# Products of constants behind the first scores of an attention and in the last step of two stacks

## The chip, the cores and the metric

The kernel runs as one program on one core of a Trainium2 chip. The metric is the device time of one execution in microseconds, the median over several runs. TensorE (PE in the rows) does the products and transposes, VectorE (DVE), ScalarE (ACT) and GpSimd (POOL) the rest; SyncE (SP) issues the transfers. TensorE's clock has two levels, 1.2 and 2.4 GHz; the profile gives it as a share of the upper one (0.50 or 1.00).

## The reference

A stream x of 8 sequences of 256 tokens by 128 features goes through four levels. Each level adds half of a feed-forward part, then an attention, then half of the same feed-forward part again:

```python
x = x + 0.5 * ffn(layernorm(x)); x = x + attn(layernorm(x)); x = x + 0.5 * ffn(layernorm(x))
```

Two parts matter here. The feed-forward part of level 2 is itself a stack of six layers, run twice in the program, before and after the attention of level 2:

```python
for i in range(6):
    x = attn_layer(shift_tokens(x), ...) + x      # 16 heads of 64, local windows of 32
    x = ffn_layer(shift_tokens(x), ...) + x       # (a * gelu(gate)) @ W2, width 341
```

The attention of level 2 is a softmax attention over all 256 tokens with 16 heads of 8 features:

```python
h = (x - mu) * rsqrt(var + 1e-5) * gamma + beta
q, k, v = split(h @ w_qkv + b_qkv)
attn = softmax(q @ k.T / sqrt(8))
out = residual + (attn @ v) @ w_out + b_out
```

## The kernel before

Twelve stages run one after the other, each in a block of its own, and every engine has its own instruction list, written in a fixed order by hand; semaphores tie them together. All numbers are float32. A float32 product is two matmul records in the trace; a transpose is one.

**stage_attention, level 2.** A step is one batch of 256 tokens, two tiles of 128. The eight batches are software-pipelined: `body(s)` on PE interleaves steps s-3 to s+1. Per step PE turns the normalized x (`turn_normed`, L915), projects q and k (`project`, L923) and v (`project_v`, L937), and computes the scores twice. The first scores, `first_score(step, g)` for four groups g of four heads (L963), write the PSUM tile `quad`; DVE reduces each group to the maxima, `reduce`, L1722, and as there is one `quad`, group g + 1 waits for the reduction of g. PE turns the maxima (`turn_negmax`, L980, into the tile `turn`, which the copy of v, L1683, must have left), DVE adds them to the queries (`q_aug`, L1738), and `score(step, n)`, n = 0 to 7 (L1005), writes the scores turned into the tile `duo`, two heads at a time. ACT takes the exponential of each (L1448) before the next may overwrite `duo`. `weigh` (L1024) multiplies by v; turns and the output product follow.

Three places already hold products of constants, whose result nobody reads. `warm(n)` (L973) multiplies the identity by itself n times into `duo`; it stands as `warm(6)` ahead of the loop and as `warm(1)` in each place of `body(0)` whose operation has no batch yet. `fill(n)` (L969) does it into `quad`: six times behind the turn of the maxima of the last batch, once behind each score of the last batch. `first_score(0, g)` is thus followed by the places of absent operations: eight records behind group 0, for instance. In `body(1)` the order around group 3 is `first_score(0, 3)`, `project_v(1)`, `turn_negmax(0)`, `first_score(1, 0)`, `score(0, 0)`.

**stage_stack.** A step is one batch in one layer, 48 steps, software-pipelined over four; `tail()` writes out the last four by hand. The last step's feed-forward part has nothing beside it: `output(last)` (L2847, 16 records), `turn_out(6)` (L2890, two transposes of batch 6 that leaves the stack), `to_tokens(last)` (L2854) once DVE has added the residual into `zc`, DVE and POOL for the statistics and the normalized `fxn`, `turn_normed(last)` (L2860), ACT for `fxnT` and the load of gelu's table, then for each of three chunks `up` (L2872), gelu on ACT (L3204), a multiplication on DVE (L3655), and `down` (L2879), whose result leaves through `turn_out(7)` (L2890) to x on DVE (L3671). The PSUM tile `score_psum` is not used any more at that point. `up`'s next chunk waits for the multiplication of the one before.

Of the kernel before, what the change touches and what calls it, by code (L numbers as in the profile page):

```python
# [21 lines left out]
P = 128  # L22
D = 128
B, SEQ = 8, 256
# [820 lines left out]
def stage_attention(chip, level):  # L845
    nc, sig, once = chip.nc, chip.loop, chip.once
# [9 lines left out]
    with ExitStack() as ctx:  # L856
        sb = lambda name, shape, dt=F32: ctx.enter_context(nc.sbuf_tensor(chip.tag + name, shape, dt))
        ps = lambda name, shape: ctx.enter_context(nc.psum_tensor(chip.tag + name, shape, F32))
        pack = sb("pack", [P, sum(width for _, width in ATTN_PARTS[level])])
        tiles = views(pack, ATTN_PARTS[level])  # L860
        if not softmax:
# [42 lines left out]
        def _(pe):  # L904
# [35 lines left out]
            def first_score(step, g):  # L940

                if softmax and g % 2 == 0:
                    pe.wait_ge(*sig("heads", step, g // 2 + 1))
                elif g == 0:
                    pe.wait_ge(*sig("k_heads", step, 1))
                pe.wait_ge(*sig(drained, step, g))
                if cut:
                    for j in range(GROUPS):
                        nc.tensor.matmul(kinds2(quad[:, j, :])[:, :, 0:P], ident_bf[:, :],
                                         mask[:, :].rearrange("p (o s) -> p o s", o=1).to_broadcast([P, T, P]),  # L950
                                         start=True, stop=False, skip_group_check=True)
                for t in range(T):
                    for j in range(GROUPS):
                        band = slice(BAND * j, BAND * (j + 1))
                        if softmax:
                            query, key = q_heads[band, step % ROOM, g, :], k_heads[band, step % ROOM, g, :]
                        else:
                            query, key = flat[band, step % ROOM, 0, :], k_heads[band, step % ROOM, 0, g, :]
                        if cut:
                            ins = nc.tensor.matmul(quad[:, j, t * P:(2 * t + 1) * P], query[:, t * P:(t + 1) * P],  # L960
                                                   key[:, 0:(t + 1) * P], start=False, stop=True, skip_group_check=True)
                        else:
                            ins = nc.tensor.matmul(quad[:, j, t * SEQ:(t + 1) * SEQ], query[:, t * P:(t + 1) * P], key,  # L963
                                                   start=True, stop=True, skip_group_check=True)
                ins.then_inc(sig["first_scores"], 1)

            def fill(count):
                for n in range(count):
                    nc.tensor.matmul(quad[:, n % GROUPS, 0:P], chip.ident[:, :], chip.ident[:, :], start=True, stop=True, skip_group_check=True)  # L969
# [5 lines left out]
            def turn_negmax(step):  # L975
                if step == 0:
                    pe.wait_ge(*once("set", 1))
                pe.wait_ge(*sig("negmax", step, GROUPS))
                for t in range(T):
                    ins = nc.tensor.transpose(turn[:, t * P:(t + 1) * P], negmax[:, t, :], chip.ident[:, :])  # L980
                ins.then_inc(sig["negmaxT"], 1)
                if step == B - 1:
                    fill(6)

            def score(step, n):
# [65 lines left out]
            if level == 0:  # L1051
                def body(s):
# [20 lines left out]
                    if runs(s + 1):  # L1073
                        bank_free(("xT", s + 3, 1), ("context", s - 1, 1))
                        turn_negmax(s + 1)
                    elif s == -2:
                        warm(1)
                    if runs(s + 2):
                        first_score(s + 2, 0)
                    elif s == -2:  # L1080
                        warm(1)
# [19 lines left out]
                    if runs(s + 2):  # L1101
                        first_score(s + 2, 1)
                    elif s == -2:
                        warm(1)
# [24 lines left out]
                    if runs(s + 2):  # L1129
                        first_score(s + 2, 2)  # L1130
                    elif s == -2:
                        warm(1)
# [34 lines left out]
            elif level == 2:  # L1167
                def body(s):
# [38 lines left out]
                    if runs(s - 1):  # L1207
                        bank_free(("v", s, 1), ("ctxT", s - 3, 1))
                        turn_negmax(s - 1)
                    elif s == 0:  # L1210
                        warm(1)
# [1331 lines left out]
def stage_stack(chip):  # L2543
# [9 lines left out]
    nc, dram, att, layer_sig, once = chip.nc, chip.dram, chip.loop, chip.layer, chip.once  # L2553
    once.use(dict(set=3, loaded=64, tables=DEPTH, primed=2))
    with ExitStack() as ctx:
# [33 lines left out]
        wide, score_psum = ps("wide", [P, 2, 512]), ps("score_psum", [P, 2, 512])  # L2589
# [165 lines left out]
        def _(pe):  # L2755
# [84 lines left out]
            def output(step):  # L2840


                pe.wait_ge(*att("ctxT", step, 4))
                pe.wait_ge(*att("z", step + B))
                pe.wait_ge(*layer_sig("wo", layer_of(step), 16))
                for c in range(LPAIRS):
                    ins = nc.tensor.matmul(out_psum, wo[:, c, :], ctxT[:, c, :], start=c == 0, stop=c == LPAIRS - 1)  # L2847
                ins.then_inc(att["out_psum"], 1)

            def to_tokens(step):  # L2850

                pe.wait_ge(*att("zc", step, 2))
                for t in range(HALVES):
                    ins = nc.tensor.transpose(f_psum[:, t * P:(t + 1) * P], zc[:, t * P:(t + 1) * P], chip.ident[:, :])  # L2854
                ins.then_inc(att["fxs_psum"], 1)

            def turn_normed(step):
                pe.wait_ge(*att("xn", step, 1))
                for t in range(HALVES):
                    ins = nc.tensor.transpose(f_psum[:, t * P:(t + 1) * P], fxn[:, t, :], chip.ident[:, :])  # L2860
                ins.then_inc(att["fxnT_psum"], 1)

            def up(step, c):

                if c == 0:
                    pe.wait_ge(*att("fxnT", step, 1))
                    pe.wait_ge(*layer_sig("ffn", layer_of(step), 48))
                else:
                    pe.wait_ge(*att("hidden", step, c))
                for half in range(2):  # L2870
                    at = half * FF + c * P
                    ins = nc.tensor.matmul(up_psum[0:width(c), half, :], w1[:, at:at + width(c)], fxnT[:, :], start=True, stop=True)  # L2872
                ins.then_inc(att["h_psum"], 1)

            def down(step):

                pe.wait_ge(*att("hidden", step, FF_CHUNKS))
                for c in range(FF_CHUNKS):
                    ins = nc.tensor.matmul(out_psum, w2[0:width(c), c, :], hidden[0:width(c), c, :],  # L2879
                                           start=c == 0, stop=c == FF_CHUNKS - 1)  # L2880
                ins.then_inc(att["f_psum"], 1)

            def turn_out(b):
                if b == 0:
                    pe.wait_ge(*att("v", STEPS - 1, HALVES))
                pe.wait_ge(att["leave"], att.base["leave"] + b + 1)
                if b > 1:
                    pe.wait_ge(att["left"], att.base["left"] + b - 1)
                for t in range(HALVES):
                    ins = nc.tensor.transpose(wide[:, b % 2, t * P:(t + 1) * P], straight[:, b % 4, t * P:(t + 1) * P], chip.ident[:, :])  # L2890
                ins.then_inc(att["tok"], 1)
# [94 lines left out]
            def tail():  # L2986
# [66 lines left out]
                turn_probs(second, 3)  # L3053
                weigh(second, 2)
                turn_out(0)
                turn_normed(third)
                turn_out(1)
                turn_free(("qkT", last, 4))
                turn_qk(last, 4)
                turn_out(2)  # L3060
                up(third, 0)
                turn_out(3)
# [46 lines left out]
                weigh(last, 7)  # L3109
                output(last)  # L3110
                turn_out(6)
                to_tokens(last)
                turn_normed(last)
                up(last, 0)
                up(last, 1)
                up(last, 2)
                down(last)
                turn_out(7)

# [3 lines left out]
            with pe.Fori(2, STEPS - 2) as s:  # L3123
                body(s)
            tail()

        @block.scalar
# [851 lines left out]
```

## Time and profile before

| what | us |
|---|---|
| median of 3 runs | 5163.54 |
| lowest and highest | 5163.06, 5172.06 |
| the profiled execution | 5160.11 |
| its span in the trace | 5158.3 |
| PE busy | 4911.5 |
| DVE busy | 3883.5 |
| ACT busy | 3435.8 |
| POOL busy | 2884.5 |

The span runs from the first to the last instruction. Busy times overlap, and a busy PE isn't one at its peak: a record's length depends on the granted clock. The idle time in brackets in a timeline is that of the engine in front of the instruction, with what it waited for.

### The profile page before, as it was taken

The numbers are of one execution on the slowest core, as the hardware profiler recorded it, in microseconds if no ns is written. First come the engines' busy times: TensorE is split into PE (matmuls) and PEld (weight loads), VectorE is DVE, ScalarE is ACT, GpSimd is POOL, SyncE is SP. The second block draws the span as 40 slices with busy tenths as digits, with TensorE's granted clock in tenths as the row PEclk, the third lists the DMA queues.
The fourth block names the chain that finished last, engine by engine and source line by source line (L and its number), as shares of the span: only waits on it lengthen the run. The fifth ranks groups of instructions, "written<-read, shape, count | busy, mean of one in ns | idle before, by whom it ended". The sixth has DMA issues, their size and how long they took to land. (4 is left out here: it accounts for less than half of the span.)

```text
span 5158.3 us, 142024 instructions
## 1 busy us (share of the span) xinstructions
PE 4911.5 (95%) x49396; PEld 3459.2 (67%) x49396; DVE 3883.5 (75%) x7068; ACT 3435.8 (67%) x5890; POOL 2884.5 (56%) x3477
## 2 busy tenths in 40 slices
PE   9989988699999999999979699999999999989999
PEld 6666656377777777777756377777777777756656
DVE  3274347699999999999856489989999989855655
ACT  3353334488888888888846478888888888852652
POOL 0010025688888888888720488888887888720200
PEclk9999999799999999999979799999999999989999
DMA  1000000112121112111100112111211111110000
GB/s 45 1 6 35 1 8 3 53 40 61 43 61 49 51 49 56 53 53 52 40 16 2 42 45 57 49 55 47 57 53 51 51 54 53 40 42 1 8 26 9
DMA packets 110503, 195.62 MB, mean 38 GB/s; under 512 B 21456, under 2 KB 28896, under 8 KB 110304
## 3 DMA queue, kind: packets, MB, share of 16 engines
q1 hardware_dynamic: 110304, 192.89, 13.3%
q8 instruction: 134, 2.20, 0.2%
q14 instruction: 65, 0.53, 0.0%
HBM read 53.36 MB, written 1.05 MB: 11 GB/s over the span
## 5 line engine op out<-in xcount | busy, mean ns | idle before, releaser
L3433 POOL TENSOR_TENSOR stage_qk<-stage_halves 128x1024 f32<-128x1024 f32 x384 | 907.7, 2364 | 17.0 <-DVE stage_halves L3591 1.9
L3469 POOL TENSOR_TENSOR stage_qk<-stage_qk,stage_rnorm 128x1024 f32<-128x1024 f32 x384 | 730.5, 1902 | 8.1 <-POOL stage_rnorm L3458 0.2
L3462 POOL TENSOR_TENSOR stage_probs<-stage_probs,stage_rsum 128x768 f32<-128x768 f32 x384 | 564.4, 1470 | 263.9 <-DVE stage_rsum L3620 263.9
L3184 ACT ACTIVATE stage_probsT<-stage_flip 96x512 f32<-96x512 f32 x768 | 452.3, 589 | 219.2 <-PE stage_flip L2821 218.5
L3588 DVE TENSOR_TENSOR stage_halves<-stage_wide,stage_tables 128x1024 f32<-128x1024 f32 x384 | 469.3, 1222 | 145.1 <-ACT stage_square L3138 94.2
L3591 DVE TENSOR_TENSOR stage_halves<-stage_wide,stage_tables 128x512 f32<-128x512 f32 x768 | 490.7, 680 | 0.0
L3600 DVE TENSOR_REDUCE stage_norm<-stage_square 128x16 f32<-128x1024 f32 x384 | 463.8, 1208 | 32.4 <-issue 32.3
L3138 ACT ACTIVATE stage_square<-stage_wide 128x1024 f32<-128x1024 f32 x384 | 393.2, 1024 | 141.1 <-PE stage_wide L2769 136.4
L2786 PE MATMUL stage_turn<-ident,stage_qk 128*128 128x128 f32 x3072 | 480.6, 279 | 6.5 <-ACT stage_qkT L3158 6.5
L2821 PE MATMUL stage_flip<-ident,stage_probs 128*96 128x128 f32 x3072 | 469.5, 275 | 7.9 <-POOL stage_probs L3462 6.9
L2835 PE MATMUL stage_pv<-stage_probsT,stage_v_win 96*64 96x64 f32 x12288 | 464.8, 226 | 2.5 <-ACT stage_ctxT L3191 1.5
L3158 ACT ACTIVATE stage_qkT<-stage_turn 128x512 f32<-128x512 f32 x768 | 454.3, 592 | 15.9 <-PE stage_turn L2786 14.1
L2835 PEld LDWEIGHTS stage_pv<-stage_probsT,stage_v_win 96*64 96x64 f32 x12288 | 397.7, 138 | 90.3 <-issue 86.3
L2821 PEld LDWEIGHTS stage_flip<-ident,stage_probs 128*96 128x96 f32 x3072 | 343.4, 126 | 167.0 <-issue 79.6
L2786 PEld LDWEIGHTS stage_turn<-ident,stage_qk 128*128 128x128 f32 x3072 | 353.9, 142 | 139.0 <-issue 85.4
L707 DVE SCALAR_TENSOR_TENSOR stage_mixes<-stage_o_psum,stage_routes,stage_mixes 128x128 f32<-128x128 f32 x480 | 135.2, 344 | 347.5 <-PE stage_o_psum L529 320.0
L3611 DVE TENSOR_TENSOR stage_shifted<-stage_score_psum,stage_negmax 128x768 f32<-128x768 f32 x384 | 367.6, 957 | 36.5
L2769 PE MATMUL stage_wide<-stage_wq,stage_xsT 128*128 128x512 f32 x768 | 380.2, 618 | 11.6 <-DVE stage_halves L3591 7.3
L2769 PE MATMUL stage_wide<-stage_wk,stage_xsT 128*128 128x512 f32 x768 | 372.6, 609 | 17.7 <-DVE stage_halves L3591 17.6
L529 PEld LDWEIGHTS stage_o_psum<-stage_w_down,stage_hidden 128*128 128x128 f32 x3072 | 359.6, 192 | 42.0 <-issue 41.1
L516 PE MATMUL stage_h_psum<-stage_xT,stage_w_up 128*128 128x512 f32 x768 | 384.0, 612 | 1.8 <-DMA stage_w_down<-in_L_w_down 1.1
L2769 PE MATMUL stage_wide<-stage_wv,stage_xsT 128*128 128x512 f32 x768 | 369.0, 604 | 7.8 <-DVE stage_halves L3591 5.5
(311 smaller groups left out, 10017.7 us busy)
## 6 DMA issues: line engine op xcount, KB each, us to landing
stage_v_win<-stage_v SPq DMA_DIRECT2D x384, 192.0 KB, 2.5
stage_v_win<-stage_v SPq DMA_DIRECT2D x384, 128.0 KB, 2.4
stage_v_win<-stage_v SPq DMA_DIRECT2D x192, 64.0 KB, 2.2
stage_wq<-in_T_wq SPq DMA_DIRECT2D x12, 512.0 KB, 4.1
stage_wk<-in_T_wk SPq DMA_DIRECT2D x12, 512.0 KB, 4.8
stage_wv<-in_T_wv SPq DMA_DIRECT2D x12, 512.0 KB, 3.4
stage_wo<-in_T_wo SPq DMA_DIRECT2D x12, 512.0 KB, 3.5
stage_w_up<-in_L_w_up SPq DMA_DIRECT2D x8, 512.0 KB, 7.1
```

What stands on the lines that cost most here:

```text
L2769: ins = nc.tensor.matmul(wide[:, c, :], xsT[:, (n % HALVES) * P:(n % HALVES + 1) * P], weights[name][:, c * 512:(c + 1) * 512], start=True ...
L2786: ins = nc.tensor.transpose(turn[:, j * P:(j + 1) * P], qk[:, chunk, pair * P:(pair + 1) * P], chip.ident[:, :])
L2821: ins = nc.tensor.transpose(flip[0:REACH, (2 * h + t) * P:(2 * h + t + 1) * P], probs[:, (n // 2) % 2, h, (n % 2) * HALVES + t, :], chip.i ...
L2835: ins = nc.tensor.matmul(pv[h * LD:(h + 1) * LD, n % 2, block * QBLOCK:(block + 1) * QBLOCK], v_win[:, block, 2 * n + h, :], probsT[:, n % ...
L3158: nc.scalar.activation(target, tiles4(turn), ACT.Copy).then_inc(att["qkT"], 1)
L3184: nc.scalar.activation(probsT[:, n % 2].rearrange("p h t q -> p (h t) q"), tiles4(flip)[0:REACH], ACT.Copy)\
L3433: nc.gpsimd.tensor_tensor(qk[:, n, :], halves[:, n % 2, 0, :], halves[:, n % 2, 1, :], ALU.add)\
L3462: nc.gpsimd.tensor_tensor(probs[:, m % 2], probs[:, m % 2], rsum[:, m % 2].to_broadcast([P, 2, 2 * HALVES, REACH]), ALU.mult)\
L3469: nc.gpsimd.tensor_tensor(heads, heads, rnorm[:, n, :].rearrange("p (h o) -> p h o", o=1).to_broadcast([P, LH, LD]), ALU.mult).then_inc(at ...
L3588: nc.vector.tensor_tensor(out[:, 0], heads, cos.to_broadcast([P, LH, LD]), ALU.mult)
L3591: ins = nc.vector.tensor_tensor(out[:, 1, :, to], heads[:, :, source], sin[:, :, to].to_broadcast([P, LH, LD // 2]), ALU.mult)
L3600: nc.vector.tensor_reduce(norm2[:, n, :], square[:, n % 2, :].rearrange("p (h d) -> p h d", d=LD), AX.X, ALU.add)\
```

## The change

Three edits, all of them added products of the identity by itself. In the attention of level 2, for the first batch only, `warm` runs 6, 2, 8 and 8 times behind the four groups of first scores, and `fill(6)` behind the turn of its maxima, as it did for the last batch. In the stack a function `fill` of the same kind, into `score_psum`, is called six times in the last step of `tail()`, 25 products in all.

```diff
@@ stage_attention, PE: first_score(step, g)
                 ins.then_inc(sig["first_scores"], 1)
+                if level == 2 and step == 0:
+                    warm((6, 2, 8, 8)[g])
@@ stage_attention, PE: turn_negmax(step)
                 ins.then_inc(sig["negmaxT"], 1)
-                if step == B - 1:
+                if step == B - 1 or level == 2 and step == 0:
                     fill(6)
@@ stage_stack, PE
+            def fill(count):
+                for n in range(count):
+                    nc.tensor.matmul(score_psum[:, n % 2, 0:P], chip.ident[:, :], chip.ident[:, :], start=True, stop=True, skip_group_check=True)
@@ stage_stack, PE: tail()
                 turn_out(6)
+                fill(4)
                 to_tokens(last)
+                fill(10)
                 turn_normed(last)
+                fill(3)
                 up(last, 0)
+                fill(3)
                 up(last, 1)
+                fill(3)
                 up(last, 2)
+                fill(2)
                 down(last)
                 turn_out(7)
```

## Rows read from the trace of the kernel before

**Rows 1.** The page: busy time by engine, and the granted clock in 40 slices.

```profile
PE 4911.5 (95%) x49396; PEld 3459.2 (67%) x49396; DVE 3883.5 (75%) x7068; ACT 3435.8 (67%) x5890; POOL 2884.5 (56%) x3477
...
PEclk9999999799999999999979799999999999989999
```

**Rows 2.** Busy time in stretches: length, each engine's busy us, PEclk, DMA share, GB/s.

```profile
2624.00:2640.00 16.00, 9.77 (x20) 5.37 (x20) 3.14 (x7) 4.96 (x7) 0.00 (x0) 0.50 0.00 0
...
2668.00:2712.00 44.00, 38.84 (x221) 23.61 (x220) 22.01 (x40) 14.12 (x19) 4.36 (x7) 0.50 0.00 1
...
4576.00:4593.00 17.00, 9.77 (x20) 5.38 (x20) 3.14 (x7) 5.15 (x8) 0.69 (x1) 0.50 0.00 0
```

**Rows 3.** Timeline, last step of the first stack: start, length, instruction, records, idle before.

```profile
2620.49 0.38 PE L2890 MATMUL stage_wide<-ident,stage_square 128*128 128x128 f32 x2
...
2621.62 0.44 PE L2854 MATMUL stage_f_psum<-ident,stage_zc 128*128 128x128 f32 x2 [0.75 <-DVE stage_zc L3628]
...
2624.78 0.69 PE L2860 MATMUL stage_f_psum<-ident,stage_fxn 128*128 128x128 f32 x2 [2.72 <-DVE stage_fxn L3647]
...
2626.09 1.28 ACT L3204 ACT_TABLE_LOAD   x1
...
2626.12 2.07 PE L2872 MATMUL stage_f_psum<-stage_fxnT,stage_w 128*128 128x256 f32 x4 [0.65 <-ACT stage_fxnT L3198]
...
2635.58 2.93 PE L2879 MATMUL stage_f_psum<-stage_hidden,stage_w 128*128 128x256 f32 x6 [1.08 <-DVE stage_hidden L3655]
...
2640.48 0.69 PE L2890 MATMUL stage_wide<-ident,stage_square 128*128 128x128 f32 x2 [1.97 <-ACT stage_square L3216]
```

**Rows 4.** The same timeline of PE, the same products one step earlier.

```profile
2609.43 1.03 PE L2872 MATMUL stage_f_psum<-stage_fxnT,stage_w 128*128 128x256 f32 x4
...
2614.05 1.56 PE L2879 MATMUL stage_f_psum<-stage_hidden,stage_w 128*128 128x256 f32 x6
```

**Rows 5.** Timeline of PE and DVE, level 2 attention, first batch.

```profile
2642.16 2.90 PE L973 MATMUL stage_duo<-ident 128*128 128x128 f32 x12 [1.00 <-PEq L2555]
...
2659.33 1.15 PE L963 MATMUL stage_quad<-stage_k_heads,stage_q_heads 32*128 32x256 f32 x16 [1.39 <-DVE stage_negmax L1722]
...
2660.68 1.06 PE L973 MATMUL stage_duo<-ident 128*128 128x128 f32 x8
...
2662.99 1.15 PE L963 MATMUL stage_quad<-stage_k_heads,stage_q_heads 32*128 32x256 f32 x16 [0.29 <-DVE stage_negmax L1722]
...
2666.54 1.15 PE L963 MATMUL stage_quad<-stage_k_heads,stage_q_heads 32*128 32x256 f32 x16 [1.76 <-DVE stage_negmax L1722]
...
2667.75 2.29 DVE L1722 TENSOR_REDUCE stage_negmax<-stage_quad 128x8 f32<-128x2048 f32 x1 [0.28 <-PE stage_quad L963]
...
2669.96 0.41 DVE L1683 TENSOR_TENSOR stage_v<-stage_turn,stage_pack 128x256 f32<-128x256 f32 x1
...
2670.43 0.69 PE L980 MATMUL stage_turn<-ident,stage_negmax 128*128 128x128 f32 x2 [1.79 <-DVE stage_v L1683]
...
2672.91 1.92 PE L1005 MATMUL stage_duo<-stage_q_aug,stage_k_heads 32*128 32x256 f32 x8
...
2675.95 0.80 PE L1005 MATMUL stage_duo<-stage_q_aug,stage_k_heads 32*128 32x256 f32 x2 [1.12 <-ACT stage_probs L1448]
...
2685.49 2.08 PE L923 MATMUL stage_pvT<-stage_xT,stage_pack 128*128 128x256 f32 x4
...
2692.40 0.80 PE L1005 MATMUL stage_duo<-stage_q_aug,stage_k_heads 32*128 32x256 f32 x2 [1.12 <-ACT stage_probs L1448]
```

**Rows 6.** Timeline of PE, level 2 attention, scores of the last batch.

```profile
2845.62 1.13 PE L1005 MATMUL stage_duo<-stage_q_aug,stage_k_heads 32*128 32x256 f32 x8
...
2847.88 1.25 PE L1005 MATMUL stage_duo<-stage_q_aug,stage_k_heads 32*128 32x256 f32 x8 [0.70 <-ACT stage_probs L1448]
...
2850.64 2.08 PE L1005 MATMUL stage_duo<-stage_q_aug,stage_k_heads 32*128 32x256 f32 x8
```

**Rows 7.** Timeline of PE, level 0 attention, a score of the first batch.

```profile
297.11 0.92 PE L1005 MATMUL stage_duo<-stage_q_aug,stage_k_heads 32*128 32x256 f32 x8 [0.91 <-ACT stage_probs L1448]
```

## The prediction, made before the changed kernel ran

> **What bounds the kernel now.** I read the page first, for the share of each engine and the row of the granted TensorE clock [rows 1]. TensorE is busy 95% of the span, so where its work is dense its speed sets the time. The clock row is below 9 tenths in a few slices only; I took those apart with the view by stretches [rows 2], then followed the instructions in order of time through the three places that the diff touches: the last step of each stack, and the first batch of the level 2 attention.
>
> Two kinds of lost time stand there. First, the end of a stack: in 2624 to 2640 and again in 4576 to 4593 the granted clock is 0.50, the lower of the two levels, 1.2 GHz [rows 2]. That step is one chain: a product, an activation, a vector operation, the next product, nothing beside it, so each product at half speed lengthens the program by its excess. Second, the attention: the clock is at 0.50 from about 2668 to 2712, with PE busy 38.84 of the 44 us [rows 2]. Around 2668 the engine had done little: it had idled 1.76 us in front of the fourth group of first scores and 1.79 us in front of the turn of the maxima [rows 5]. Before the fall in the stack it had idled 0.75 us, done two turns, and was in a pause of 2.72 us [rows 3].
>
> **The price of a filler.** One product of a filler is two records of a 128x128 float product. At half level 12 records take 2.90 us, at full level 8 take 1.06 us with the pipeline's tail [rows 5]; without the tail (0.42 and 0.27) that is about 0.22 and 0.11 us a record, so 0.43 and 0.23 us a filler.
>
> **The stacks' last step.** It gets 25 fillers, 50 records, in six places, all in pauses.
> - fill(4), 0.91 us at full level, starts behind the two turns issued at 2620.49, so near 2620.71, and ends near 2621.62, exactly where to_tokens started when DVE released it [rows 3]. Cost 0, with nothing to spare.
> - fill(10), 2.3 us, goes into the pause of 2.72 us [rows 3]: cost 0.
> - fill(3) before up 0: 0.68 us into 0.65 us of pause and the 0.25 us by which the turns shorten. fill(3) twice and fill(2) before up 1, up 2 and down: 0.68, 0.68 and 0.46 us into pauses of 1.1 us, as in front of down [rows 3]. Cost 0 at full level.
>
> What they buy is the full level for what follows. The same products at full level stand a few microseconds earlier [rows 4]: the two turns 0.44 for 0.69, four records of up 1.03 for 2.07, six of down 1.56 for 2.93 [rows 3]. So: turns 0.25; up 0 1.04, but the load of the activation table (1.28 us, 2626.09 to 2627.37) is now late next: it starts with the turns' 0.25 us gain at 2625.84, ends at 2627.12, and holds the gelu that began at 2628.23, so turns and up 0 together give 1.1; up 1 and up 2 about 1.0 each, down 1.37, the last turn 0.25. Sum 4.7 us. If the last turn, which stands behind two more microseconds of idle, is back at half level, 4.5. Two stacks: 9.2 us. Bounds: nothing if the level falls all the same, 9.4 if it holds to the end.
>
> **The attention's start.** All of it moves 4.7 us earlier. Its head runs at half level today up to about 2654 and I leave that; whether the level comes back a little earlier or later against the work is open, for the products that run meanwhile (about six fillers and a projection) ±1 us. I put +0.5.
>
> **More products behind first scores.** The four groups are spaced by first score, reduction of 2.29 us on DVE, next first score. warm(6) behind group 0 is 12 records, 1.37 us, in a pause of 1.39 us plus the tail of the old eight (0.27): cost 0. warm(2) behind group 1, 0.46 us, delays project(1), but PE had 0.29 us and the tail before group 2 [rows 5]: at most 0.1. warm(8) behind group 2, 1.83 us, in 1.76 us plus 0.27: 0 to 0.1. warm(8) behind group 3 is in front of project_v(1): its four records now start 1.8 us later, at 2669.4, and end near 2670.0, where the copy of v on DVE began at 2669.96 [rows 5] behind the reduction. Cost 0.1 or 0.2, since the turn of the maxima waits for that copy. fill(6), 1.37 us, stands in front of first_score(1, 0), and so of its reduction, and of score(0, 0); with turn and first_score at full level (0.4 and 1.15 us, against 2.5 us now from turn to score) score(0, 0) starts at about 2673.2 instead of 2672.91. So nothing is won up to here, 0.3 lost.
>
> **Behind them.** Now it counts how long the level holds. The scores of batch 0 go through one pair of banks: score, a pause of 1.12 us for the exponential, next score [rows 5]; a score at full level is 1.13 us, as in rows 6. So score(0, 0) at 2673.2, score(0, 1) at 2675.4 (was 2675.95, 0.6 won). first_score(1, 1) and a turn, 2.3 us with it, cover the next wait: score(0, 2) at 2677.7, score(0, 3) at 2679.9, project(2) at 2680.9 (was 2685.49, 4.6 won). project(2) 1.0, first_score(1, 2) 1.1 and score(0, 4) 1.1 reach 2684.0, and a pause 2685.1 with score(0, 5) (was 2692.40, 7.3 won). Between these scores stand pauses of about 1.2 us, in front of scores 1, 3 and 5, with no filler in them, and a score uses 32 of the 128 rows. The nearest row: late in the same attention, at full level, two scores with a filler and a pause of 0.70 us between them, and the level falls within the second (1.25 us; the next one 2.08) [rows 6]. Against it: in the level 0 attention a pause of 0.91 us between two such scores, and they stay short [rows 7]. The pauses here are longer than both. So the likeliest is that the level falls again in one of them; I take the middle one, 4.6 us, ends 0.6 and 7.3. From there the work is at half level as before, and comes back where it does now.
>
> The Trainium skill (TensorE: Matmul & The Clock Gate, section A second HAM failure mode: psum-queue depth-cycling) says that small idle times between groups of matmuls that cycle through PSUM buffers make the gate swing between its levels. By that rule the scores of the first batch fall again, as rows 6 show once. The same page's closing table (Why this matters for your kernels) asks only that no long idle stand between bursts; by that rule today's fall near 2668, with no pause above 1.79 us [rows 5], would not be there, so the trace disagrees; it would give the second rival's time.
>
> **Sum.** -9.2 (stacks), +0.5 (start), +0.3 and -4.6 (first batch) is -13.0 us. On the profiled execution, 5160.11 us (its span 5158.3 and 1.8 around it), that is 5147. The median of the runs, 5163.54, is 3.4 above the profiled one, so 5150.5; I predict 5150.
>
> **Rivals.**
> 1. *The level falls again among the first batch's scores* (the forecast): 5150, own range 5145 to 5155. Chance 0.50.
> 2. *It holds into the steady state.* 2668 to 2712 has 38.8 us of busy PE at half level [rows 2] and 5 us idle; at full level 19.4, with 1.4 for fill(6), three pauses of 1.2 and some 2.5 of start and tails: 27 for 44, so -17 less 0.3. With the stacks -25: 5138. For it: rows 7. Against it: rows 6. Chance 0.22.
> 3. *Little arrives.* The level falls in the stack's end despite fill(4) and fill(10), in one or both, or the head of the attention stays at half level beyond the fillers; half of the 9.2 and none to 4 us of the rest remain: 5154 to 5161, within 0.2%. For it: fill(4) has no time to spare and the level was already gone by 2624. Chance 0.20.
> 4. *The fillers run at half level and become the wait.* Then each costs 0.43 us. Behind the first scores: 2.6 less 1.4 of pause, 0.9 less 0.3, 3.4 less 1.8, 3.4 with almost none, and 2.6 for fill(6): about 10 us. In the stack 1.7 less 0.75, 4.3 less 2.7, 1.3 less 0.65, 1.15 and 1.08: about 3.4 us each. Together +17, 5180; the attention's part alone, with the stacks as forecast, gives about 5164. It decides if the level isn't back when group 1 is issued, and in both stacks is gone before fill(10). Against it: the first scores run at full level today (1.15 us a group) [rows 5]. Chance 0.05.
> The other 0.03 is effects on later stages, whose own changes of level shift with everything.
>
> **From this the numbers.** A change within 0.2%, 10.3 us, is about what can't be told from none. Faster by more: most of case 1 (0.43 of 0.50; its low end, -9.8, is just inside the bound) and all of case 2: 0.65. Within: the rest of case 1, case 3, and part of the rest: 0.29. Slower: 0.06. Range 5137 to 5160, from case 2 to most of case 3.
>
> **What would show it.** In the profile after: a granted clock near 1.00 over the 16 us in front of each stack's last turn, up at 1.03 to 1.13 us and down at 1.56 (step right), or 2.07 and 2.93 (case 3). The four first-score groups of batch 0 still 3.6 us apart, else the fillers are the wait (case 4). project_v(1) followed at once by the copy of v. Then the length of each score(0, n): 1.13 turning to 2.08 at score 1, 3 or 5 is case 1, 1.13 throughout case 2. Wrong, too, if half-level stretches move elsewhere: a tail that ends 4.7 us sooner and a later stage that gives it back.

## The result: 18 us less in the first comparison, 0.35%

| | us |
|---|---|
| before, median of 6 | 5164.16 (5163.06 to 5172.06) |
| changed, median of 6 | 5146.01 (5136.93 to 5151.52) |
| ratio, 95% interval | 0.9965 [0.9952, 0.9978] |
| the changed kernel's profiled execution, its span | 5140.83, 5139.0 |

The page of the changed kernel, the lines that answer to [rows 1]:

```profile
PE 4909.0 (96%) x49556; PEld 3465.6 (67%) x49556; DVE 3883.5 (76%) x7068; ACT 3437.8 (67%) x5890; POOL 2884.5 (56%) x3477
...
PEclk9999999799999999999999799999999999999999
```

PE is busy 2.5 us less with 160 records more (49556 for 49396): 80 products of constants were added, 30 in the attention and 25 in each stack, and others got shorter. The stretches, as in [rows 2], same columns:

```profile
2624.00:2640.00 16.00, 11.93 (x77) 9.87 (x75) 5.32 (x15) 5.38 (x8) 0.69 (x1) 1.00 0.00 1
2641.00:2655.00 14.00, 8.34 (x35) 7.35 (x36) 8.02 (x32) 3.77 (x9) 7.91 (x10) 0.52 0.12 36
...
2668.00:2712.00 44.00, 39.38 (x410) 26.92 (x409) 31.66 (x56) 25.25 (x36) 5.88 (x9) 1.00 0.01 1
4556.00:4573.00 17.00, 12.56 (x80) 10.48 (x78) 5.33 (x15) 5.38 (x8) 0.69 (x1) 1.00 0.00 0
```

Both stacks' ends and the 44 us from 2668 on are at full level in this execution. A short stretch at half level stays between them, in the head of the attention (2641 to 2655, 0.52).

The timeline of PE in the last step of the first stack, as [rows 3]:

```profile
2620.43 3.72 PE L2849 MATMUL stage_f_psum<-stage_ctxT,stage_wo 128*128 128x256 f32 x16 [0.70 <-ACT stage_ctxT L3203]
...
2624.20 1.06 PE L2887 MATMUL stage_score_psum<-ident 128*128 128x128 f32 x8
2625.12 0.44 PE L2856 MATMUL stage_f_psum<-ident,stage_zc 128*128 128x128 f32 x2
2625.39 2.40 PE L2887 MATMUL stage_score_psum<-ident 128*128 128x128 f32 x20
2628.27 0.44 PE L2862 MATMUL stage_f_psum<-ident,stage_fxn 128*128 128x128 f32 x2 [0.48 <-DVE stage_fxn L3659]
...
2629.37 1.13 PE L2874 MATMUL stage_f_psum<-stage_fxnT,stage_w 128*128 128x256 f32 x4
...
2631.74 1.13 PE L2874 MATMUL stage_f_psum<-stage_fxnT,stage_w 128*128 128x256 f32 x4 [0.58 <-DVE stage_hidden L3667]
...
2636.12 1.56 PE L2881 MATMUL stage_f_psum<-stage_hidden,stage_w 128*128 128x256 f32 x6 [0.63 <-DVE stage_hidden L3667]
2639.65 0.44 PE L2896 MATMUL stage_wide<-ident,stage_square 128*128 128x128 f32 x2 [1.96 <-ACT stage_square L3228]
```

In it, up takes 1.13 us where it took 2.07, down 1.56 for 2.93, and the last turn 0.44 for 0.69. From the start of output(last) to the start of the last turn it takes 19.22 us, and took 23.55.

The timeline of PE in the first batch of the attention, as [rows 5]:

```profile
2655.68 1.15 PE L963 MATMUL stage_quad<-stage_k_heads,stage_q_heads 32*128 32x256 f32 x16
2656.76 2.50 PE L975 MATMUL stage_duo<-ident 128*128 128x128 f32 x20
2659.30 1.15 PE L963 MATMUL stage_quad<-stage_k_heads,stage_q_heads 32*128 32x256 f32 x16
...
2666.64 1.15 PE L963 MATMUL stage_quad<-stage_k_heads,stage_q_heads 32*128 32x256 f32 x16
2667.72 2.05 PE L975 MATMUL stage_duo<-ident 128*128 128x128 f32 x16
...
2670.74 0.44 PE L982 MATMUL stage_turn<-ident,stage_negmax 128*128 128x128 f32 x2 [0.52 <-DVE stage_v L1685]
2671.01 1.50 PE L971 MATMUL stage_quad<-ident 128*128 128x128 f32 x12
...
2673.41 1.03 PE L1007 MATMUL stage_duo<-stage_q_aug,stage_k_heads 32*128 32x256 f32 x8
2675.56 0.70 PE L1007 MATMUL stage_duo<-stage_q_aug,stage_k_heads 32*128 32x256 f32 x4 [1.12 <-ACT stage_probs L1450]
...
2680.11 1.13 PE L1007 MATMUL stage_duo<-stage_q_aug,stage_k_heads 32*128 32x256 f32 x8 [1.12 <-ACT stage_probs L1450]
2681.17 1.13 PE L923 MATMUL stage_pvT<-stage_xT,stage_pack 128*128 128x256 f32 x4
```

The first two groups of first scores still start 3.62 us apart (2655.68, 2659.30): the products behind them lie in the pauses. Pauses of 1.12 us for the exponential stand in front of scores 1, 3 and 5, and no score gets longer: in this execution the level holds.

Split at landmarks that both traces have, the profiled executions differ by 19.3 us:

| from, to | before | changed | difference |
|---|---|---|---|
| start, output(last) of the first stack | 2616.93 | 2620.43 | +3.50 |
| to the last turn of that stack | 23.55 | 19.22 | -4.33 |
| to the turn of the maxima of batch 0 | 29.95 | 31.09 | +1.14 |
| to the turn of the maxima of batch 2 | 58.80 | 42.43 | -16.37 |
| to output(last) of the second stack | 1840.12 | 1840.24 | +0.12 |
| to its last turn | 23.93 | 19.61 | -4.32 |
| to the end of the span | 565.02 | 565.98 | +0.96 |

The first row holds no changed instruction. That executions of one kernel differ by microseconds in places that nobody touched is what the experiments had to deal with. Over the 14 profiled executions of this document the first output(last) starts anywhere from 2613.62 to 2631.73 us, and the stretch from the turn of the maxima of batch 2 to output(last) of the second stack takes 1835.15 to 1848.01 us, with no edit in either but e8's in the last batch. These differences are larger than any that the edits make, so single times of whole executions don't decide between the theories below; the intervals between landmarks do.

### The profile page after: what moved, and what is told of

It is laid out like the page before. It is cut to its first block and busy times, and to the rows that moved or that the text cites. A ratio compares the mean times of both kernels' runs of the same rounds, so it can differ in the third digit from the quotient of the medians.

```text
span 5139.0 us, 142344 instructions
## 1 busy us (share of the span) xinstructions
PE 4909.0 (96%) x49556; PEld 3465.6 (67%) x49556; DVE 3883.5 (76%) x7068; ACT 3437.8 (67%) x5890; POOL 2884.5 (56%) x3477
## 3 DMA queue, kind: packets, MB, share of 16 engines
q1 hardware_dynamic: 110304, 192.89, 13.4%
```

## The experiments

Two intervals are compared over all of them, read from the starts of the rows in each timeline: the **end** of a stack, from output(last) to the last turn, and the **first batches**, from the turn of the maxima of batch 0 to that of batch 2 (and to that of batch 1 where it is named). Each comes from one profiled execution and is a difference of two rounded starts, so 0.01 us means nothing. The expectations of e9 to e12 count from landmarks on DVE instead: their 21.5 and 16.9 us of a stack's end are the 23.55 and 19.22 here. Their 43.1 us, and the 25 to 28 us of the changed kernel in e12's, run from the first addition of the maxima (2671.21 in the first trace) to a reduction on DVE that starts at 2714.30. The last column is the median of the whole execution. Where it is of one run there is no verdict on the time. The runs come from three series, each with its own executions of before: median 5163.87 us of 34 for e1 to e4, 5159.89 of 19 for e5 to e8, one of 5164.18 for e9 to e12.

| kernel | end of stack 1 | end of stack 2 | first batches | us (runs) |
|---|---|---|---|---|
| before | 23.55 | 23.93 | 58.80 | 5164.16 (6) |
| e9, before again | 22.79 | 23.91 | 48.47 | 5150.91 (1) |
| e10, before a third time | 22.81 | 23.91 | 48.46 | 5150.55 (1) |
| e1, stacks only | 19.23 | 19.61 | 48.56 | 5150.41 (12) |
| e2, attention only | 23.56 | 23.64 | 44.08 | 5157.20 (12) |
| changed | 19.22 | 19.61 | 42.43 | 5146.01 (6) |
| e3, changed again | 19.23 | 19.61 | 44.08 | 5148.09 (12) |
| e4, pauses filled | 19.24 | 19.61 | 42.43 | 5141.34 (11) |
| e5, no fill(4), fill(10) | 20.42 | 20.55 | 44.08 | 5138.43 (1) |
| e6, no fill behind the maxima | 19.24 | 19.61 | 44.56 | 5147.75 (12) |
| e7, twice the stacks' fillers | 21.92 | 21.93 | 44.07 | 5153.42 (1) |
| e8, more places | 19.24 | 19.61 | 42.43 | 5139.49 (8) |
| e11, only fill(4), fill(10) | 19.23 | 21.88 | 44.07 | 5151.47 (1) |
| e12, only fill behind the maxima | 19.23 | 19.61 | 42.43 | 5136.44 (1) |

### e1 and e2: each part alone

e1 takes the attention's products out, e2 those of the stacks.

```diff
 e1, against the changed kernel
-                if level == 2 and step == 0:
-                    warm((6, 2, 8, 8)[g])
...
-                if step == B - 1 or level == 2 and step == 0:
+                if step == B - 1:
                     fill(6)
 e2, against the changed kernel: the six calls of fill in tail() removed
```

> Only the fillers in the last step of the two stacks; the level 2 attention as before. Theory A (each part by itself, as in the sum): 4.7 us for each stack at most, 4.3 as the trace after shows, so -8.6 to -9.4 us, 5154 to 5156. Theory B (the stacks' gain is given back by the attention's start, whose half-level stretch only ends later against the work): -4 or less, 5159 or more.

> Only the products behind the first scores and the maxima of the first batch of the level 2 attention; the stacks as before. Theory A (the level holds through the scores of the first batch in every execution): -15 us, 5149, in each run within 2 us. Theory B (it holds in some executions and falls again in others, as the prediction took for the likeliest): the runs spread over 10 us or more, the median between -5 and -12 us, 5152 to 5159.

e1: 5150.41 us median of 12, ratio to before 0.9983 [0.9970, 0.9995], which is 8.8 us of 5164 and what theory A expected. The ends are 19.23 and 19.61 us: both stacks win, in this execution too, and nothing of it is given back in the head (29.99 us from the last turn to the turn of the maxima, for 29.95). The median is below the expected 5154 and 13.5 us under before's (5163.87 of 34, from 5146.78 to 5173.51); the ratio isn't that of the medians, and its interval holds everything from 2.6 to 15.5 us. So the times agree with the 8.8 but don't measure it well; the ends of the stacks do.

e2: 5157.20 us median of 12, from 5147.11 to 5169.14, ratio 0.9991 [0.9978, 1.0004]: 4.6 us, alone not told from nothing. Theory A's 15 us lies outside the interval, which ends at 11.4; the size is theory B's, and its profile shows the level fall in the first batch. The spread of 22 us is not evidence for it: before itself spreads over 27. 8.8 and 4.6 make 13.4.

### e3: the changed kernel again

> The changed kernel once more, for another profiled execution and more times. Theory A (always holds): the same cold stretches in the attention as in the first trace, none between 2656 and 2832 us, times within 3 us of one another. Theory B (depends on the execution): times again spread over 10 us or more, and about half of the profiles show a score of the first batch that turns from 1.13 to 2.08 us behind a pause of 1.12 us.

5148.09 us median of 12, 5138.96 to 5162.23, ratio 0.9972 [0.9958, 0.9986], 14.5 us. That the level doesn't hold in every execution is theory B's: in the timeline of PE of this execution it falls, behind score 3 of batch 0:

```profile
2682.50 1.13 PE L1007 MATMUL stage_duo<-stage_q_aug,stage_k_heads 32*128 32x256 f32 x8 [1.12 <-ACT stage_probs L1450]
2683.56 1.49 PE L923 MATMUL stage_pvT<-stage_xT,stage_pack 128*128 128x256 f32 x4
2684.97 2.09 PE L963 MATMUL stage_quad<-stage_k_heads,stage_q_heads 32*128 32x256 f32 x16
2686.84 1.41 PE L1007 MATMUL stage_duo<-stage_q_aug,stage_k_heads 32*128 32x256 f32 x8
2689.38 0.48 PE L1007 MATMUL stage_duo<-stage_q_aug,stage_k_heads 32*128 32x256 f32 x2 [1.13 <-ACT stage_probs L1450]
```

score(0, 3) is still 1.13, project(2) is 1.49 and first_score(1, 2) 2.09 for 1.15, score(0, 4) 1.41, and the next is short again. So it falls behind two pauses of 1.12 us, as the prediction had it, but it is back within score(0, 4). The whole costs 1.65 us (44.08 for 42.43), not the rest of the way to the steady state. That is too little to make the spread of 23.3 us, which theory B laid to it: this execution's span is 11.8 us longer than the first one's, 7.8 of it between batch 2 and the second stack's last step and 3.1 ahead of the first stack's.

### e4: the pauses filled

```diff
 score(step, n), behind the increment of "scores"
+                if level == 2 and step == 0 and n in (0, 2, 4):
+                    pe.wait_ge(*(sig("xT", 2, 1) if n == 4 else sig("heads", 1, 2)))
+                    bank = turn if n == 4 else pvT.rearrange("p g s -> p (g s)")
+                    for i in range(4):
+                        nc.tensor.matmul(bank[:, 0:P], chip.ident[:, :], chip.ident[:, :], start=True, stop=True, skip_group_check=True)
```

> The changed kernel, and in the first batch four more products of constants behind scores 0, 2 and 4 (into banks that are free there), which take 0.9 of each pause of 1.12 us. Theory B (the pauses let the level fall in some executions): the spread of the times shrinks, and the median is 3 to 8 us below that of the changed kernel, 5138 to 5143. Theory A (it never falls there): the same as the changed kernel, 5146, or up to 0.5 us more for the added products.

5141.34 us median of 11, 5132.94 to 5149.69, ratio 0.9964 [0.9950, 0.9979]. The timeline of PE:

```profile
2681.06 1.03 PE L1007 MATMUL stage_duo<-stage_q_aug,stage_k_heads 32*128 32x256 f32 x8
2682.01 1.16 PE L1016 MATMUL stage_pvT<-ident 128*128 128x128 f32 x8
2683.21 0.70 PE L1007 MATMUL stage_duo<-stage_q_aug,stage_k_heads 32*128 32x256 f32 x4
```

Eight records fill the pause without delaying the next score, which again starts 2.15 us behind the one before, and the first batches take 42.43 us, the value without a fall. The median is 6.8 us under that of e3 and within what theory B expected, but the intervals of e3 and e4 overlap, and the fall that e4 avoids costs 1.65 us by the traces, so it can't be what makes the 6.8. Nor does the smaller spread (16.8 us for 23.3) say that the pauses made it: e6, with its pauses open, spreads over 15.1. What is shown is that filling the pauses costs nothing. In both executions with the pauses filled (e4, e8) the level held, and in one of the six with both edits and open pauses; that the filling makes the difference is likely, not shown.

### e9 and e10: the kernel before, two more executions

e1's unchanged attention had taken 48.56 us where the first trace of before had 58.80, which put the price of the whole attention part in doubt.

> The kernel before, once more, for another profiled execution. Theory A (the first trace is typical: the level is at half for some 44 us in the level 2 attention and 31 us from each stack's end): the first batch to the return of the level takes 43.1 us again, within 2. Theory B (how long the half level lasts there differs from one execution to the next, as the attention alone unchanged in e1 suggests, where it took 10.2 us less): another length, between 28 and 45 us; the stack's end 21.5 us again.

> The same again, a third execution. Theory B: the attention's stretch differs from the other two, while the stack's end stays at 21.5 us.

48.47 and 48.46 us; the stack's end 22.8 us, 0.75 less than in the first trace. The timeline of PE in e9:

```profile
2671.32 0.69 PE L980 MATMUL stage_turn<-ident,stage_negmax 128*128 128x128 f32 x2 [1.92 <-DVE stage_v L1683]
...
2686.38 2.08 PE L923 MATMUL stage_pvT<-stage_xT,stage_pack 128*128 128x256 f32 x4
2688.39 1.61 PE L963 MATMUL stage_quad<-stage_k_heads,stage_q_heads 32*128 32x256 f32 x16
2689.82 1.02 PE L1005 MATMUL stage_duo<-stage_q_aug,stage_k_heads 32*128 32x256 f32 x8
```

The level falls ahead of the turn of the maxima as in [rows 5] (0.69 us), already within the project_v(1) before it, and comes back within first_score(1, 2) (1.61 for 2.09), 17 us after the turn. In [rows 2] it stayed down for 44 us. Three executions of the unchanged attention (e9, e10, e1) take 48.5 us and one 58.8: what I read as the cost of the old schedule was, of these four, the longest. Theory B; but e9 and e10 do not differ from each other, and the end of the first stack did not stay as it was (22.8 for 23.55 us).

### e5, e7, e11: which filler of the stack does what

e5 drops fill(4) and fill(10), e11 drops the four later groups, e7 doubles all six.

```
 e5                      e11                     e7
-    fill(4)              (stays)                 fill(8)
-    fill(10)             (stays)                 fill(20)
     fill(3)             -    fill(3)             fill(6)
     fill(3)             -    fill(3)             fill(6)
     fill(3)             -    fill(3)             fill(6)
     fill(2)             -    fill(2)             fill(4)
```

> The changed kernel without fill(4) and fill(10) in the stacks' last step; fill(3), 3, 3 and 2 stay. Theory A (the two groups in front of the normalized x keep the level up, the others only fill): the level falls near the start of the statistics as before, up is 2.07 us again for at least the first chunk, and the products of constants at 0.43 us overrun their pauses: output(last) to the last turn takes 0 to 1 us more than before (23.5 us). Theory B (the four later groups are enough to bring the level back during up 0 or up 1): 1 to 3 us less than before, 20.5 to 22.5 us. The changed kernel took 19.2.

> The changed kernel without the four later groups in the stacks' last step; fill(4) and fill(10) stay. Theory A (the two early groups keep the level, and the chunks' own products carry it on): the end takes 16.9 us as in the changed kernel. Theory B (three chunks with pauses of 0.6 to 1.1 us between them let it fall again): up at 2.07 us from chunk 1 or 2 on, 18 to 20 us.

> The changed kernel with twice the products in the last step of the stacks: 8, 20, 6, 6, 6, 4. It prices a product at full level where no pause hides it. Theory A (0.22 us each, hidden only in what is left of each pause: 0, 0.48, 0, 0.58, 0.42, 0.63 us by the trace after): 0.9 + 1.8 + 0.7 + 0.1 + 0.3 = 3.8 us more per stack than the changed kernel, output(last) to the last turn 23.0 us. Theory B (products of constants are overlapped by the queue, or the level falls): under 2 us more, or over 6.

e5 takes 20.42 and 20.55 us. The timeline of PE, from the turn of the normalized x:

```profile
2628.81 0.69 PE L2862 MATMUL stage_f_psum<-ident,stage_fxn 128*128 128x128 f32 x2 [2.72 <-DVE stage_fxn L3657]
2629.29 1.48 PE L2887 MATMUL stage_score_psum<-ident 128*128 128x128 f32 x6
2630.57 1.73 PE L2874 MATMUL stage_f_psum<-stage_fxnT,stage_w 128*128 128x256 f32 x4
2632.14 0.83 PE L2887 MATMUL stage_score_psum<-ident 128*128 128x128 f32 x6
```

The level has fallen (turn 0.69, six records 1.48), but fill(3), up and fill(3) leave PE no pause, and it is back within up 0 (1.73). So the two early groups are worth 1.2 and 0.9 us on top of the later ones, which bring most of the gain alone: theory B, whose 20.5 to 22.5 us it meets within 0.1.

e11 takes 19.23 us in the first stack and 21.88 in the second. In the second, timeline of PE:

```profile
4572.31 1.13 PE L2874 MATMUL stage_f_psum<-stage_fxnT,stage_w 128*128 128x256 f32 x4 [1.24 <-DVE stage_hidden L3663]
4574.52 2.00 PE L2874 MATMUL stage_f_psum<-stage_fxnT,stage_w 128*85 128x256 f32 x4 [1.08 <-DVE stage_hidden L3663]
4577.60 2.93 PE L2881 MATMUL stage_f_psum<-stage_hidden,stage_w 128*128 128x256 f32 x6 [1.08 <-DVE stage_hidden L3663]
```

up 1 takes 1.13, up 2 takes 2.00: the level falls between them, behind pauses of 1.24 and 1.08 us. In one stack the early groups suffice, in the other they don't; with the later groups the level held in both stacks in all eight profiled executions that have the six groups (changed, e1, e3, e4, e6, e7, e8, e12). Each theory is right in one of the two stacks.

e7 takes 21.92 and 21.93 us, 2.7 and 2.3 more than the changed kernel. The timeline of PE:

```profile
2624.72 4.63 PE L2887 MATMUL stage_score_psum<-ident 128*128 128x128 f32 x40
2629.19 0.38 PE L2862 MATMUL stage_f_psum<-ident,stage_fxn 128*128 128x128 f32 x2
...
2637.34 1.56 PE L2881 MATMUL stage_f_psum<-stage_hidden,stage_w 128*128 128x256 f32 x6 [0.18 <-DVE stage_hidden L3667]
```

40 records take 4.63 us, 0.11 each, and delay the turn by what sticks out of the pause. In front of down 0.18 us of idle is left, so the last three groups stay hidden even when doubled. The sum expected by theory A was 3.8, and neither theory has 2.7 and 2.3. In the first stack 0.9 and 1.5 came at the first two groups (0.88, and 1.53 for 1.8), 0.46 at the third, and nothing after; up 0 gave 0.17 back. A filler at full level outside a pause costs 0.22 us, as priced.

### e6 and e12: the attention's two edits apart

```diff
 e6, against the changed kernel
-                if step == B - 1 or level == 2 and step == 0:
+                if step == B - 1:
                     fill(6)
 e12, against the changed kernel
-                if level == 2 and step == 0:
-                    warm((6, 2, 8, 8)[g])
```

> The changed kernel without fill(6) behind the maxima of the first batch; the 24 products behind the first scores stay. Theory A (the products behind the first scores carry the level over and fill(6) only stands in front of the next group): the first batch's scores start 1.1 to 1.4 us earlier and the level holds as often: 0 to 1.4 us faster than the changed kernel. Theory B (fill(6) is needed in the stretch of the turn of the maxima): the level falls more often in the pauses before scores 1 and 3, median 1 to 4 us slower than the changed kernel.

> The changed kernel without the 24 products behind the first scores; fill(6) behind the maxima stays. Theory A (the fall comes in the pauses of the first scores, so fill(6) is issued at half level and takes 2.6 us): the first batch to the steady state 25 to 28 us becomes 38 us or more, near the kernel before. Theory B (fill(6) brings the level back within one group): 28 to 33 us.

e6: 5147.75 us median of 12, ratio 0.9983 [0.9972, 0.9993], against e3's 0.9972 [0.9958, 0.9986], each to before of its own series: not told apart. Its stretches, columns as in [rows 2]:

```profile
2677.00:2681.00 4.00, 2.85 (x28) 1.86 (x30) 3.92 (x7) 1.02 (x1) 1.36 (x2) 1.00 0.00 0
2681.00:2685.00 4.00, 4.00 (x30) 2.85 (x30) 2.13 (x7) 1.31 (x2) 0.70 (x1) 0.57 0.01 4
...
2688.00:2692.00 4.00, 4.00 (x26) 2.88 (x26) 0.14 (x1) 2.95 (x5) 0.00 (x0) 0.57 0.00 0
```

The level falls twice (0.57 in 2681 to 2685 and in 2688 to 2692). score(0, 0) starts 1.46 us behind the turn, 1.2 sooner than with fill(6), and still the first batches take 44.56 us, 0.5 more than with one fall. A trade of 1.2 us for another fall of the level, in one execution.

e12 went against both expectations. The timeline of PE:

```profile
2659.24 1.15 PE L963 MATMUL stage_quad<-stage_k_heads,stage_q_heads 32*128 32x256 f32 x16 [1.76 <-DVE stage_negmax L1722]
...
2663.13 0.44 PE L980 MATMUL stage_turn<-ident,stage_negmax 128*128 128x128 f32 x2 [2.10 <-DVE stage_v L1683]
2663.40 1.50 PE L969 MATMUL stage_quad<-ident 128*128 128x128 f32 x12
```

With the old pauses, 1.76 us and 2.10 us, the turn is 0.44 us and fill(6) 1.50: the level had not fallen. The first batches take 42.43 us, the best value, without one of the 24 products behind the first scores. One execution doesn't tell how often; it shows that those products are not necessary each time. Nor can fill(6) have kept the level up to the turn, behind which it stands: ahead of the turn, e1 has the same instructions, and there it had fallen (0.69). What the products do shows over all profiled executions. With them the turn of the maxima takes 0.44 us in nine of nine (changed, e2 to e8, e11), e2 with the old stacks among them; without them 0.69 in four (before, e9, e10, e1) and 0.44 in one (e12).

### e8: more places

e4, and fill(3) for fill(1) behind scores 1 and 3 of the last batch, warm(15) for warm(6) ahead of the attention's loop, fill(6) between down and the last turn of each stack.

```diff
-                    fill(1)
+                    fill(3 if level == 2 and n in (1, 3) else 1)
...
-            warm(6)
+            warm(15 if level == 2 else 6)
...
                 down(last)
+                fill(6)
                 turn_out(7)
```

> The changed kernel with the pauses of the first batch filled as in e4, two more products behind scores 1 and 3 of the last batch, warm(15) for warm(6) ahead of the attention's loop, and fill(6) between down and the last turn of each stack. Theory A (each half-level stretch that is left near these places shortens): the last turn at full level in each stack, 0.2 us each; the attention's head 1 to 2 us shorter, since project(0) and the products behind it run at full level; the last batch without its stretch at half level, 1 to 7 us: median 2 to 6 us under e4's 5141.3. Theory B (the head is bound by VectorE and ScalarE and the last batch by the exponentials): the same as e4 within 2 us.

5139.49 us median of 8, 5129.68 to 5148.65, ratio 0.9962 [0.9948, 0.9975]: the lowest median, and not told apart from e4 or from the changed kernel. In its profile the scores of the last batch are all 1.13 us, with pauses of 0.26 where [rows 6] have 0.70. But e2, whose last batch is the old one with its pause of 0.70, shows the same; the sixth of the eight scores, in the timeline of PE of e2 and of e8:

```profile
2850.96 1.13 PE L1007 MATMUL stage_duo<-stage_q_aug,stage_k_heads 32*128 32x256 f32 x8 [0.27 <-ACT stage_probs L1450]
...
2845.29 1.13 PE L1007 MATMUL stage_duo<-stage_q_aug,stage_k_heads 32*128 32x256 f32 x8 [0.27 <-ACT stage_probs L1455]
```

From the first to the last of the eight scores it is 17.99 us in e2, e5 and e8, and 20.8 or 22.3 in the other eleven executions, where the sixth score takes 2.07 or 2.08. So holding the level there is worth at least 2.8 us, and it also comes without e8's products; whether they make it more frequent is open. The ends of the stacks and the first batches are those of e4, so neither fill(6) nor warm(15) shows anything; theory B for these two.

## Why the prediction was right, and where not

The time, 5146, lies in the range and in the direction that was forecast, 4 us under the 5150. The stacks' part came as worked out; that the attention's part brought the sum so near is luck, by two errors that cancel.

**The stacks' last step: right in mechanism and size.** 4.7 us a stack were worked out, 0.25 of it for the last turn itself. From output(last) to the start of the last turn 4.33 and 4.32 were won, and the turn shortened by the 0.25: 4.6. Against e9 and e10 the first stack wins 3.6 and not 4.3, as the level fell later there: its turn of the normalized x took 0.44 us. fill(4) does end where to_tokens starts (2625.12), the level stays up, and the activation table's load is the thing next late: up 1 comes 1.09 us sooner against the turn of the normalized x, where 1.1 was said. The timeline of ACT after, where gelu follows the load at once:

```profile
2629.33 1.28 ACT L3216 ACT_TABLE_LOAD   x1
2630.63 0.47 ACT L3216 ACTIVATE stage_gelu<-stage_f_psum,stage_cols 128x256 f32<-128x256 f32 x1
```

**The attention's head: right.** +0.5 with ±1 around it; +1.14 in this pair of traces; in the other executions the stretch takes 29.8 to 31.1 us, for 29.95 to 30.08 in the three of before. In the changed kernel's first trace the level came back later against the work, so project_v ran at 1.06 us and the last warm products at 1.22.

**The products behind the first scores: right as costs, and they do hold the level.** Groups 3.62, 3.78 and 3.56 us apart, the middle one 0.12 later as the 0.1 of the sum has it, project_v(1) followed at once by the copy of v, score(0, 0) 2.67 us behind the turn for 2.8. The turn of the maxima is at full level in nine of nine executions with them and in one of five without. The prediction names the 1.79 us in front of the turn as idle time before the fall, but the level had already gone in the project_v(1) ahead of that pause, as the timeline of PE before shows (1.02 us, 0.61 after):

```profile
2667.61 1.02 PE L937 MATMUL stage_turn<-stage_pack,stage_xT 128*128 128x128 f32 x4
```

So of the pauses named only the 1.76 us came before it.

**The chain behind them: right.** project(2) at 2681.17 is 7.76 us behind score(0, 0); 7.7 was worked out.

**The step that failed, although the time came right,** is "From there the work is at half level as before, and comes back where it does now." The level did fall in the pauses where the prediction put it: e3 shows it, and e2, e5, e7 and e11 have the same length, 44.07 or 44.08 us. That is five of the six profiled executions with both edits of the attention and nothing in its pauses; the sixth, the first one, held. But the level came back within a few microseconds, and a fall cost 1.65 us. The prediction priced it by the 44 us of the first trace, at which a fall at project(2) would have left some 12 us of the 17 lost.

**A second error cancelled most of it.** The same first trace gave the old attention 58.80 us between the landmarks, where three other executions take 48.5. Against those, the attention part wins 4.4 us with one fall and 6.0 without; rival 2's 17 us (16.4 in the first pair of traces) is the difference from the one long case. With 7.9 to 9.2 for the stacks, by which trace of before one takes, that makes 12 to 15, less up to 1.1 in the head, which agrees with 14.5 in e3 and with 13.4 from e1 and e2. The 18 us of the first comparison are within its interval, 11 to 25; its other 3 or more are not accounted for by any interval here. So the median was nearly hit by a price for the attention (4.3 net) that is about the 4.4 of an execution with a fall, through two steps that were each some 10 us off.

**Chances.** By what the level did in the first batch, the first profiled execution is rival 2 (holds) and five later ones (e2, e3, e5, e7, e11) are the forecast (falls again); the six times of the comparison, 5136.93 to 5151.52, cover the times of both, 5138 and 5150, so they don't choose. Rival 3 did not come: both stacks win in every profiled execution with the six groups. Of rival 4 nothing is seen in the changed kernel: its fillers in the stacks and behind the first scores ran at full level; e7 gives the price where they leave the pause.

The Trainium skill (TensorE: Matmul & The Clock Gate, section A second HAM failure mode: psum-queue depth-cycling) was right to warn of small idle times: e3 shows such a fall. Its closing table, which asks for no long idle only, isn't borne out: in e9 the level falls within project_v(1), and the longest PE pause since the first group of first scores is 1.76 us. The page also says, in its section What's actually happening, that how many products run at the lower level at a kernel's start varies from run to run of one kernel; e9 against the first trace shows the like in the middle of a kernel, with 48.5 and 58.8 us for the same instructions.

## What to carry to other kernels

One trace of a stretch at half clock is one draw: before pricing it by its length, look at a second execution. The same holds for whole times: one that moves by 10 us may have done so in stretches that nobody touched, so compare intervals between landmarks. Products of constants cost nothing measurable where they fit a pause at full level, and 0.22 us each where they don't (measured by doubling them). In a serial chain, where every product behind them counts, they won 3.6 to 4.3 us a stack; where the pauses leave room their number need not be exact. In the first batches, with little idle time behind the fall, the level came back by itself 17 us after the turn in three of four executions of the old schedule, and the added products were worth 4 to 6 us; a later fall, 1.65 us.

## What the runs showed that I had not expected

- The same kernel's executions spread over 27 us of 5164 (5146.78 to 5173.51, 34 runs of before), and the identical instructions of the attention take 48.47 or 58.80 us, with another granted clock.
- Interval lengths come in few values: 42.43 without a fall, 44.07 or 44.08 with one, 48.46 to 48.56 for three of the old ones; e6, with two falls, has 44.56.
- The level came back in e5 within three dense groups (fill, up, fill) that started at half level: the fillers don't have to prevent the fall to be of use, 20.4 us for 22.8 to 23.55.
